# Four cross-attention layers on one core: folded weights stored in whole rows, prologue transfers in another order, three transposes inside the second query projection, weight pieces split in other phases

## The chip, the cores and the metric

One core of a Trainium2 chip runs the kernel. The metric is the device time of one execution in microseconds (us), as the median of several runs. TensorE (PE) multiplies matrices, VectorE (DVE), ScalarE (ACT) and GpSimd (POOL) do elementwise work, and the sync engine's queue (SP) issues most transfers.

## The reference

Four cross-attention layers follow one another on `x` (4 batches, 1024 tokens, 512 features); each attends to a context of 64 tokens of 1024 features. Layers 0 and 2 are "grouped", layers 1 and 3 are "masked":

```python
# grouped (layers 0 and 2)
xn = rmsnorm(x, norm_w)
q = (xn @ wq)                       # 16 heads of 32
k, v = cond @ wk, cond @ wv         # 4 key heads of 32
attn = softmax(q k^T / sqrt(32))
x = x + (attn v) @ wo
# masked (layers 1 and 3)
q, k, v = x @ Wq, ctx @ Wk, ctx @ Wv      # 16 heads of 64
logits = q k^T / 8 + column bias of four token positions, by mask
x = x + softmax(logits) v @ Wo + bo
```

## The kernel before

Every product of matrices that needs precision is made of three PE passes (`three`, lines 372 to 376): the operands are split into a high part (ACT, a copy that rounds to fp32r) and a low part (a subtraction on DVE or POOL), and high x high, high x low and low x high are summed. So each operand passes ACT and then DVE or POOL before PE can use it.

**Prologue.** For the masked layers the query weights are multiplied into the keys and the output weights into the values ahead of time ("folding"): 32 steps n (`MASKED`), each one projection of keys or values (`m_made`, 24 matmuls of 256 columns) and one fold (`folding`, 12 matmuls of 512 columns into four PSUM banks). ACT and DVE empty the four banks into staging buffers (`taken_out`), and SP stores them to DRAM: 256 KB each, to `s_fm` (folded query weights, n 0 to 7 and 16 to 23) or to `s_fn` (folded output weights). Staging buffers are used again two steps of a kind later, after the store has landed (`f_st`). SP issues all of it in program order: the loads of the raw weights (`w_load`, `f_load`), the grouped keys and values (`g_store`), the folded weights (`f_store`), the first block of x into `ring`. The last 8 of the 32 steps are interleaved with the first attention phase.

**Main part.** There are 8 iterations `it`: 2 layer pairs x 4 batches. Each has four phases of 8 steps u (four groups of 128 tokens x two halves of the heads): phases 0 and 1 are the grouped layer for the first and second block of 512 tokens, phases 2 and 3 the masked layer. While PE makes the scores of phase k, it also transposes the finished probabilities of phase k-1 (`transposes`, into the bank `TB`; phases 0 and 3 alternate with `MX`), multiplies them by the values (`product`), and in phases 1 and 2 adds the output projection (`out_part`, eight pieces per phase). A transposed block goes through ACT (`pt_hi`) and DVE (`pt_lo`) before its product and before `TB` can be used again. Softmax of a step: ACT copies the scores (`copied`), DVE takes the maximum (`evac`), POOL subtracts it (`less_max`), ACT takes the exponential (`exp`), DVE sums and takes the reciprocal (`sums`), POOL multiplies (`norm`); in phases 2 and 3 DVE does the first part alone.

Before phases 0 and 1 there is the query projection (`q_bound`): four chunks c of 12 matmuls; chunk c needs the chunk of x split by ACT (`x_hi`) and POOL (`x_lo`). The output weights of the grouped layer are split during phase 1: ACT `ws_hi(it, 4 + u)` after `copied(it, 1, u)`, POOL `ws_lo(it, 4 + u)` after `less_max(it, 1, u)`. `out_part` for j waits for piece j of them:

```python
                if ph == 1 and part == 0:
                    pe.wait_ge(S["ws_lo"], 8 * it + 4 + j + 1)
```

The folded weights come back in 16 pieces of 256 KB per iteration through the four slots of `ring`, and are split by `part_hi` (ACT) and `part_lo` (DVE for pieces 0 to 3, POOL for the others): pieces 0 to 3 are used by steps u 0 to 3 of phases 2 and 3, pieces 4 to 7 by steps u 4 to 7, pieces 8 to 15 by the products of phase 3 and of the next phase 0. After phase 1, DVE adds the layer's output to x (`xnew`), ACT and then POOL and DVE split it (`xb_hi`, `xb_lo`), and the scores of phase 2 (`scores(it, 2, 0)`) need all four chunks of it.

Each engine works through its own program in order; the order of the calls in the code below is therefore the order of the work on that engine. PE's iterations 1 to 7 are one hardware loop.

## Time and profile before

| | |
|---|---|
| median of 3 runs | 1669.56 us (1668.48 to 1671.2) |
| profiled execution, its own time | 1669.71 us |
| span in the profile | 1667.9 us |
| mean granted clock of TensorE | 0.995 of full speed |
| PE busy | 1597.5 us (96%) |
| DVE, POOL, ACT busy | 1089.3, 882.1, 769.7 us |

The profile is of one execution. The span is what the trace covers; the execution's own time is 1.8 us longer. Matmuls are pipelined and their ends are modelled, so a matmul of 512 columns shows about 0.39 us while the next one starts 0.23 us after it: an idle time before a matmul is therefore about 0.16 us shorter in the records than the lateness of its start.

### The profile page before, as it was taken

What the parts mean: (1) busy time and instruction counts of PE and PEld (TensorE: products, weight loads), DVE (VectorE), ACT (ScalarE), POOL (GpSimd) and SP (SyncE); (2) the same over time, 40 slices, a digit from 0 to 9 for tenths busy, and PEclk for the clock granted to TensorE, in tenths of its full rate; (3) what the DMA queues carried; (4) which work ended last, traced back from release to release, by engine and by line L of the source; (5) the groups of instructions that cost most, each with busy time, mean ns of one, the idle gap of its engine ahead of it and who ended that gap; (6) DMA issues with size and microseconds to landing.
All of it is one profiled execution on the core that took longest, in us unless ns stands there. A gap on an engine that the chain in (4) does not pass through costs nothing.

```text
span 1667.9 us, 25208 instructions
## 1 busy us (share of the span) xinstructions
PE 1597.5 (96%) x8160; PEld 1330.8 (80%) x8160; DVE 1089.3 (65%) x1825; ACT 769.7 (46%) x1353; POOL 882.1 (53%) x809
## 2 busy tenths in 40 slices
PE   7999999999999999999999999999999999999998
PEld 6988887788778877878777877887787877787786
DVE  6676468764676567655876567656865587657764
ACT  4565566334643364435642463336533563246331
POOL 4040446645745575556755575557455665557430
PEclk9999999999999999999999999999999999999999
DMA  9999562121311222121222231122112221222101
GB/s 321 276 341 339 187 228 89 51 68 67 132 39 52 102 83 76 45 96 61 105 57 65 77 120 40 50 102 95 64 51 90 82 89 51 65 76 95 43 9 51
DMA packets 118451, 172.18 MB, mean 103 GB/s; under 512 B 35760, under 2 KB 69040, under 8 KB 112176
## 3 DMA queue, kind: packets, MB, share of 16 engines
q1 hardware_dynamic: 115424, 153.16, 28.1%
q10 hardware_dynamic: 2736, 16.78, 2.5%
q8 instruction: 78, 1.28, 0.3%
q14 instruction: 53, 0.43, 0.1%
q0 software_dynamic: 160, 0.53, 0.1%
HBM read 118.53 MB, written 51.91 MB: 102 GB/s over the span
## 4 chain that ended last, share of the span: by engine, by line
PE 45%; issue 25%; POOL 17%; DVE 5%; ACT 4%; SPq 2%; DMA 2%; POOLq 0%; DVEq 0%; ACTq 0%
PE OB L374 10%; PE OB L376 9%; PE OB L375 9%; POOL foldN L1243 4%; PE SB L374 3%; PE SB L376 3%; PE SB L375 3%; PE TB L488 2%; POOL xqhl L1228 2%; POOL xhl L1249 2%; POOL foldM L1243 2%; POOL wqo L1146 2%; POOL wraw L1139 1%; POOL prob L1220 1%; DVE pT L905 1%
## 5 line engine op out<-in xcount | busy, mean ns | idle before, releaser
L1220 POOL TENSOR_TENSOR prob<-prob,small 128x512 f32<-128x512 f32 x256 | 281.4, 1102 | 392.4 <-DVE small L1023 392.4
L775 ACT ACTIVATE pT<-TB 128x512 fp32r<-128x512 f32 x192 | 114.0, 594 | 280.3 <-PE TB L488 280.3
L1004 DVE SCALAR_TENSOR_TENSOR prob<-SB,aux 128x512 f32<-128x512 f32 x128 | 88.2, 689 | 198.3 <-PE SB L376 198.3
L1214 POOL TENSOR_TENSOR prob<-prob,small 128x512 f32<-128x512 f32 x128 | 133.9, 1046 | 151.3 <-DVE small L998 151.3
L374 PE MATMUL SB<-foldM,xhl 128*128 128x512 f32 x512 | 202.0, 395 | 9.0 <-POOL foldM L1243 6.9
L374 PE MATMUL OB<-pT,foldN 128*128 128x512 f32 x512 | 205.8, 402 | 3.8 <-DVE pT L905 3.7
L905 DVE TENSOR_TENSOR pT<-TB,pT 128x512 fp32r<-128x512 f32 x192 | 127.9, 666 | 117.4 <-ACT pT L775 116.8
L375 PE MATMUL OB<-pT,foldN 128*128 128x512 f32 x512 | 200.5, 392 | 0.0
L376 PE MATMUL OB<-pT,foldN 128*128 128x512 f32 x512 | 200.4, 391 | 0.0
L376 PE MATMUL SB<-foldM,xhl 128*128 128x512 f32 x512 | 199.7, 390 | 0.0
L375 PE MATMUL SB<-foldM,xhl 128*128 128x512 f32 x512 | 199.3, 389 | 0.0
L998 DVE TENSOR_REDUCE small<-prob 128x8 f32<-128x512 f32 x128 | 87.4, 683 | 137.2 <-ACT prob L768 136.2
L747 ACT ACTIVATE prob<-prob 128x512 f32<-128x512 f32 x128 | 80.9, 632 | 207.5 <-DVE prob L1010 206.8
L768 ACT ACTIVATE prob<-SB 128x512 f32<-128x512 f32 x128 | 76.5, 598 | 167.0 <-PE SB L376 166.9
L488 PE MATMUL TB<-ident,prob 128*128 128x128 f32 x768 | 117.5, 275 | 18.1 <-DVE pT L905 18.0
L374 PEld LDWEIGHTS SB<-foldM,xhl 128*128 128x128 f32 x512 | 96.1, 188 | 38.7 <-POOL foldM L1243 10.2
L488 PEld LDWEIGHTS TB<-ident,prob 128*128 128x128 f32 x768 | 90.3, 140 | 43.5 <-DVE pT L905 25.7
L374 PE MATMUL OB<-xqhl,wqo 128*128 128x512 f32 x256 | 105.6, 412 | 17.4 <-POOL xqhl L1228 16.1
L1228 POOL TENSOR_TENSOR xqhl<-ring,xqhl 128x512 fp32r<-128x512 f32 x64 | 82.2, 1295 | 66.1 <-ACT xqhl L754 66.0
L374 PEld LDWEIGHTS OB<-pT,foldN 128*128 128x128 f32 x512 | 96.7, 189 | 22.0 <-DVE pT L905 4.0
L376 PEld LDWEIGHTS OB<-pT,foldN 128*128 128x128 f32 x512 | 96.5, 189 | 21.1
L376 PEld LDWEIGHTS SB<-foldM,xhl 128*128 128x128 f32 x512 | 96.1, 188 | 20.4
(159 smaller groups left out, 4121.8 us busy)
## 6 DMA issues: line engine op xcount, KB each, us to landing
prob<-in_wkvM_dram SPq DMA_DIRECT2D x32, 512.0 KB, 5.7
ring<-s_fm SPq DMA_DIRECT2D x64, 256.0 KB, 2.6
ring<-s_fn SPq DMA_DIRECT2D x64, 256.0 KB, 2.6
out_dram<-x ACTq DMA_DIRECT2D x15, 1024.0 KB, 3.9
wraw<-in_wqG_dram SPq DMA_DIRECT2D x8, 1024.0 KB, 4.8
s_fm<-prob SPq DMA_DIRECT2D x32, 256.0 KB, 5.5
s_fn<-x SPq DMA_DIRECT2D x32, 256.0 KB, 5.0
ring<-in_xT_dram SPq DMA_DIRECT2D x32, 256.0 KB, 3.2
```

Of the source, the lines that this page charges most:

```text
L374: pe.matmul(out, a_hi, b_hi, start=start, stop=False)
L375: pe.matmul(out, a_hi, b_lo, start=False, stop=False)
L376: return pe.matmul(out, a_lo, b_hi, start=False, stop=stop)
L488: last = pe.transpose(out[:, tt * P:(tt + 1) * P], pr[:, tt, t * P:(t + 1) * P], ident[:, :])
L775: act.activation(pT[:, t % 2, 0, :], t_bank(ph, t)[:, :], ACT.Copy).then_inc(S["pt_hi"], 1)
L905: return dve.tensor_tensor(out, psum, hi.bitcast(F32), ALU.subtract)
L998: dve.reduce_max(hmax[u % 2], own, AX_X).then_inc(S["maxed"], 1)
L1004: dve.scalar_tensor_tensor(out=own, in0=bank, scalar=M_SCALE, in1=row, op0=ALU.mult, op1=ALU.add).then_inc(S["biased"], 1)
L1214: pool.tensor_tensor(own, own, hmax[u % 2].unsqueeze(2).broadcast_to([P, HH, KEYS]), ALU.subtract).then_inc(S["evac"], 1)
L1220: pool.tensor_tensor(own, own, rsum[u % 2].unsqueeze(2).broadcast_to([P, HH, KEYS]), ALU.mult).then_inc(S["normed"], 1)
L1228: pool.tensor_tensor(xqhl[:, 1, c % 2, :], ring[:, c, :], xqhl[:, 0, c % 2, :].bitcast(F32), ALU.subtract).then_inc(S["x_lo"], 1)
L1243: pool.tensor_tensor(fold_part(i, 1), ring[:, i % 4, :], fold_part(i, 0).bitcast(F32), ALU.subtract).then_inc(S["fb_lo"], 1)
```

## The change

- The folded query weights are stored to `s_fm` with each partition's 2 KB in one piece (before: four pieces of 512 bytes); they are read back as pieces of 512 bytes instead of whole rows.
- In the prologue SP issues the loads in another order: two of the first four `f_load`s and the query weights `wraw` later, `w_load(4)` and `w_load(5)` ahead of the grouped stores, the first block of x at n = 20 instead of 24. ACT splits the query weights at n 12 to 15 (before 8 to 11) and the first two chunks of x at n = 20.
- In the second query projection PE makes transposes 0, 1, 2 ahead of chunks 1, 2, 3, and products 0 and 1 ahead of chunks 2 and 3. Phase 1 then starts with its scores, and from u = 1 makes transpose u+2, product u+1 and output piece u-1. The first transpose of phase 2 moves ahead of the last scores of phase 1.
- In iterations 1 to 7 weight pieces 0 to 3 are loaded before the second block of x and split in phase 0 (before: phase 1); pieces 4 to 7 are loaded ahead of the next query weights and split two at a time at the start of phase 2, and the scaling of the next query weights moves up.
- POOL: `norm(it, 3, 5)` moves behind the first two `x_lo` of the next iteration, and `x_lo(it, 1, 2)` ahead of `norm(it, 0, 7)`.

The core of the diff:

```diff
-        sFM = nc.dram_tensor("s_fm", (PAIRS, BATCH, 2, DC, P, HALF), F32, kind="Internal").ap()
+        sFM = nc.dram_tensor("s_fm", (PAIRS, KC, DC, P, BATCH, P), F32, kind="Internal").ap()
...
-                        sp.dma_start(sFM[lp, :, t // 4, o, :, (t % 4) * P:(t % 4 + 1) * P].rearrange("b p n -> p b n"),
-                                     staged(n, o).rearrange("p (b n) -> p b n", b=BATCH)).then_inc(f_st[n % 2], 16)
+                        sp.dma_start(sFM[lp, t, o].rearrange("p b n -> p (b n)"), staged(n, o)).then_inc(f_st[n % 2], 16)
...
             for n in range(4):
                 w_load(n)
-                f_load(n)
+                if n < 2:
+                    f_load(n)
...
-            sp.dma_start(wraw[:, :, :], wqG[0]).then_inc(S["ld_w"], 16)
-            for i in range(GROUP):
-                g_store(0, i)
-            for n in range(2):
-                sp.dma_start(wG[:, n], wkvG[1, n]).then_inc(wg_in[n], 16)
             for n in range(4, MASKED + 9):
                 if n < MASKED:
                     w_load(n)
+                if n == 5:
+                    for i in range(GROUP):
+                        g_store(0, i)
+                    for i in range(2):
+                        sp.dma_start(wG[:, i], wkvG[1, i]).then_inc(wg_in[i], 16)
+                    f_load(2)
+                    f_load(3)
...
+                if n == 11:
+                    sp.dma_start(wraw[:, :, :], wqG[0]).then_inc(S["ld_w"], 16)
...
-                if n == 24:
+                if n == 20:
                     sp.wait_ge(f_st[0], 4 * 64)
...
+                def half(hf, c):
+                    return sFM[lp, 4 * hf:4 * hf + 4, c, :, b, :].rearrange("t p n -> p t n")
...
                     for c in range(DC):
-                        ring_load(4 + c, x_of(1)[:, c, :])
+                        half_load(0, c, ("x_lo", value(8, c + 1)), ("x_sq", value(8, c + 1)))
                     sp.wait_ge(S["stored0"], value(16))
                     sp.dma_start(X[0][:, :, :], x_of(0)).then_inc(S["ld_x0"], 16)
-                for c in range(DC):
-                    ring_load(8 + c, sFM[lp, b, 0, c])
+                    for c in range(DC):
+                        ring_load(c, x_of(1)[:, c, :], ("fa_lo", value(4, c + 1)))
...
                 sp.dma_start(X[1][:, :, :], x_of(1)).then_inc(S["ld_x1"], 16)
+                for c in range(DC):
+                    if first:
+                        half_load(1, c, ("fa_lo", c + 1))
+                    else:
+                        half_load(1, c, ("x_lo", value(8, c + 5)), ("x_sq", value(8, c + 5)))
...
 # tensor engine, q_bound
                 for c in range(DC):
-                    if c == DC - 1 and not (first and ph == 0):
-                        transposes(it, ph, 0, first)
-                        if ph == 0:
-                            transposes(it, ph, 1, first)
+                    if ph == 1 and c > 0:
+                        transposes(it, 1, c - 1, first)
+                        if c > 1:
+                            product(it, 1, c - 2, first)
+                    elif c == DC - 1 and not first:
+                        transposes(it, 0, 0, first)
+                        transposes(it, 0, 1, first)
...
             def grouped_grouped(it, first):
 
-                for u in range(STEPS):
-                    if u > 0:
-                        transposes(it, 1, u, first)
-                        product(it, 1, u - 1, first)
-                    if u >= 3:
-                        out_part(it, 1, (u - 3) // 2, (u - 3) % 2)
+                scores(it, 1, 0, first)
+                for u in range(1, STEPS):
+                    if u + 2 < KC:
+                        transposes(it, 1, u + 2, first)
+                    if u + 1 < KC:
+                        product(it, 1, u + 1, first)
+                        out_part(it, 1, (u - 1) // 2, (u - 1) % 2)
+                    if u == STEPS - 1:
+                        transposes(it, 2, 0, first)
                     scores(it, 1, u, first)
-                product(it, 1, KC - 1, first)
-                out_part(it, 1, 2, 1)
-                transposes(it, 2, 0, first)
                 out_part(it, 1, 3, 0)
                 out_part(it, 1, 3, 1)
...
 # scalar engine: prologue, phase 0, phase 1, phase 2
-                if 8 <= n < 8 + DC:
-                    ws_hi(0, n - 8)
+                if 12 <= n < 12 + DC:
+                    ws_hi(0, n - 12)
+                if n == 20:
+                    for i in range(PAIRS):
+                        act.wait_ge(g_st[i], (BATCH + 2) * 16)
+                    act.wait_ge(S["bias_b"], PAIRS)
+                    x_hi(0, 0, 0, True)
+                    x_hi(0, 0, 1, True)
...
+                    if not first and u < 4:
+                        part_hi(it, u, first)
...
+                copied(it, 1, 0)
+                ws_hi(it, DC)
+                for u in range(1, STEPS):
+                    if u + 2 < KC:
+                        pt_hi(it, 1, u + 2)
+                    if u % 2 == 0:
+                        ot_hi(2 * it, u // 2)
+                    if u == STEPS - 1:
+                        pt_hi(it, 2, 0)
                     copied(it, 1, u)
-                    if u == STEPS - 1:
-                        ot_hi(2 * it, 3)
-                    if u > 0:
-                        exp(it, 1, u - 1)
+                    exp(it, 1, u - 1)
                     if u < DC:
                         ws_hi(it, DC + u)
...
-                    part_hi(it, 4 + s - 1)
+                    if s <= 2:
+                        part_hi(it, 2 + 2 * s, first)
+                        part_hi(it, 3 + 2 * s, first)
+                    elif s <= 6:
+                        part_hi(it, 5 + s, first)
...
 # vector engine: phase 0, phase 1
+                    if not first and u < 4:
+                        part_lo(it, u)
...
                 pt_lo(it, 1, 0)
+                pt_lo(it, 1, 1)
+                pt_lo(it, 1, 2)
+                ot_lo(2 * it, 0)
                 q_lo(it, 1)
...
+                    if u == STEPS - 1:
+                        pt_lo(it, 2, 0)
                     evac(it, 1, u, first)
-                    if u == STEPS - 1:
-                        ot_lo(2 * it, 3)
-                    if u > 0:
-                        sums(it, 1, u - 1, first)
-                    if 3 <= u < 3 + DC:
+                    sums(it, 1, u - 1, first)
+                    if first and 3 <= u < 3 + DC:
                         part_lo(it, u - 3)
-                pt_lo(it, 2, 0)
...
 # gpsimd
                 if not first:
+                    norm(it - 1, 3, STEPS - 3)
                     norm(it - 1, 3, STEPS - 2)
...
+                x_lo(it, 1, 2, first)
                 norm(it, 0, STEPS - 1)
-
-                x_lo(it, 1, 2, first)
...
-                for u in range(STEPS):
-                    part_lo(it, 4 + u)
-                    if u >= DC and nxt is not None:
-                        ws_scale(it + 1, u - DC, nxt)
-                    if u < STEPS - 2:
-                        norm(it, 2, u)
+                for u in range(STEPS - 2):
+                    if u < 2:
+                        part_lo(it, 4 + 2 * u)
+                        part_lo(it, 5 + 2 * u)
+                    else:
+                        part_lo(it, 6 + u)
+                        if nxt is not None:
+                            ws_scale(it + 1, u - 2, nxt)
+                    norm(it, 2, u)
```

## Rows read from the trace of the kernel before

**Rows 1.** The page, busy time of each engine and share of the span.
```profile
PE 1597.5 (96%) x8160; PEld 1330.8 (80%) x8160; DVE 1089.3 (65%) x1825; ACT 769.7 (46%) x1353; POOL 882.1 (53%) x809
```

**Rows 2.** Waits of PE: line, releaser, us in total, times, longest.
```profile
PE TB L488 <- DVE pT L905: 18.0, 40, 0.7
PE OB L374 <- POOL xqhl L1228: 16.1, 15, 3.0
...
PE SB L374 <- POOL foldM L1243: 6.9, 8, 0.9
```

**Rows 3.** Timeline of PE, prologue: start, us, engine, line; in brackets idle before and releaser.
```profile
32.14 0.47 PE L374 MATMUL OB<-foldM,pT 128*128 128x512 f32 x1 [3.61 <-ACT ring L696]
...
165.76 0.47 PE L374 MATMUL OB<-foldM,pT 128*128 128x512 f32 x1 [1.88 <-ACT x L696]
...
173.38 0.75 PE L374 MATMUL OB<-xqhl,wqo 128*128 128x512 f32 x1 [3.04 <-POOL xqhl L1228]
```

**Rows 4.** Timeline of SP, prologue: the issues of four weight loads.
```profile
20.81 3.02 SPq L202 DMA_DIRECT2D prob<-in_wkvM_dram  x4
```

**Rows 5.** Timeline of ACT, prologue.
```profile
27.92 1.06 ACT L670 ACTIVATE foldN<-prob 128x1024 fp32r<-128x1024 f32 x1 [7.08 <-DMA prob<-in_wkvM_dram]
...
165.01 1.09 ACT L696 ACTIVATE x<-OB 128x512 f32<-128x512 f32 x2 [1.94 <-DMA s_fm<-x]
```

**Rows 6.** Windows: us busy, instructions of PE, PEld, DVE, ACT, POOL; clock; DMA share; GB/s.
```profile
100.00:130.00 30.00, 29.29 (x190) 26.63 (x189) 21.13 (x31) 16.08 (x29) 10.76 (x19) 1.00 0.98 331
130.00:175.00 45.00, 39.53 (x225) 34.29 (x224) 27.26 (x41) 24.70 (x45) 3.14 (x3) 0.94 1.07 337
```

**Rows 7.** Windows behind two stalls of PE, columns as in group 6.
```profile
33.47:36.88 3.41, 3.41 (x10) 2.54 (x9) 3.37 (x6) 2.42 (x5) 3.24 (x8) 0.50 0.92 250
...
1453.42:1456.83 3.41, 3.41 (x9) 2.63 (x9) 2.32 (x5) 0.63 (x1) 1.95 (x3) 0.50 0.31 96
```

**Rows 8.** Timeline of PE at two starts of an iteration.
```profile
1093.25 0.49 PE L374 MATMUL OB<-xqhl,wqo 128*128 128x512 f32 x1 [1.95 <-POOL xqhl L1228]
...
1453.14 0.59 PE L374 MATMUL OB<-xqhl,wqo 128*128 128x512 f32 x1 [1.91 <-POOL xqhl L1228]
```

**Rows 9.** Timeline of PE, iteration 3, start of phase 1.
```profile
789.62 0.37 PE L374 MATMUL SB<-kG,foldM 128*128 128x256 f32 x1
...
790.77 0.48 PE L374 MATMUL MX<-pT,vG 128*128 128x512 f32 x1
791.56 0.28 PE L374 MATMUL SB<-kG,foldM 128*128 128x256 f32 x1
...
793.00 0.66 PE L488 MATMUL TB<-ident,prob 128*128 128x128 f32 x4 [0.59 <-DVE pT L905]
...
797.25 0.40 PE L374 MATMUL OB<-foldN,wqo 128*128 128x512 f32 x1
```

**Rows 10.** Timeline of all engines, the same stretch: what POOL does.
```profile
792.13 1.04 POOL L1214 TENSOR_TENSOR prob<-prob,small 128x512 f32<-128x512 f32 x1 [0.80 <-DVE small L998]
...
793.13 1.29 POOL L1146 TENSOR_TENSOR wqo<-wraw,wqo 128x512 fp32r<-128x512 f32 x1
```

**Rows 11.** The page's costliest groups: busy, mean ns of one, idle before.
```profile
L775 ACT ACTIVATE pT<-TB 128x512 fp32r<-128x512 f32 x192 | 114.0, 594 | 280.3 <-PE TB L488 280.3
...
L1214 POOL TENSOR_TENSOR prob<-prob,small 128x512 f32<-128x512 f32 x128 | 133.9, 1046 | 151.3 <-DVE small L998 151.3
...
L905 DVE TENSOR_TENSOR pT<-TB,pT 128x512 fp32r<-128x512 f32 x192 | 127.9, 666 | 117.4 <-ACT pT L775 116.8
```

**Rows 12.** Timeline of all engines, end of phase 1 of iteration 3.
```profile
818.08 2.47 DVE L1034 TENSOR_TENSOR x<-OB,x 128x512 f32<-128x512 f32 x4
...
819.50 3.01 POOL L1249 TENSOR_TENSOR xhl<-x,xhl 128x512 fp32r<-128x512 f32 x2 [1.18 <-ACT xhl L789]
...
820.86 0.50 PE L374 MATMUL SB<-foldM,xhl 128*128 128x512 f32 x1 [0.15 <-POOL xhl L1249]
```

**Rows 13.** Timeline of PE in phase 2 of iteration 3.
```profile
844.48 0.50 PE L374 MATMUL SB<-foldM,xhl 128*128 128x512 f32 x1 [0.85 <-POOL foldM L1243]
```

More of the change, by code:

```diff
@@ L696, in taken_out, with x_hi @@
                     act.activation(staged(n, o), FB[o][:, :], ACT.Copy).then_inc(S["ev_a"], 1)
+            def x_hi(it, ph, c, first):
+                a = 2 * it + ph
+                act.wait_ge(ld_ring[c], 16 * (6 * it + (ph + 1 if first else 2 * ph + 1)))
+                if not (first and ph == 0 and c < 2):
+                    act.wait_ge(S["qchunk"], 4 * a + c - 1)
+                act.activation(xqhl[:, 0, c % 2, :], ring[:, c, :], ACT.Copy).then_inc(S["x_hi"], 1)
+                if c >= 2:
+                    act.wait_ge(S["sq_added"], 3 * a + 1)
+                elif not (first and ph == 0):
+                    act.wait_ge(S["sq_added"], 3 * a - 1 + c)
+                act.activation(xsq[:, c % 2, :], ring[:, c, :], ACT.Square).then_inc(S["x_sq"], 1)
             def ws_hi(it, i):
```

87 lines of the change are left out of this document (35 added, 52 removed).

## The prediction, made before the changed kernel ran

> **What bounds the kernel.** The page's busy times come first: PE is busy 96% of the span, no other engine over 65% [rows 1]. So the end is set by PE's instructions, which the change leaves the same in number and shape, and by the moments in which PE waits. I then read PE's waits in total, and where in an iteration each stands. Three groups matter: transposes that wait for the low part of the block before them (18.0 us), query projections that wait for x from POOL (16.1 us), and scores that wait for folded weights from POOL (6.9 us) [rows 2]. A wait costs more than its idle time, since about 0.16 us hide behind the modelled end of the matmul before it.
>
> The second loss is the clock. After the 3.61 us wait at 32.14 [rows 3] a stretch of 3.41 us ran at half speed, 1.2 instead of 2.4 GHz, and so did one behind the 1.91 us wait at 1453.14 [rows 7, 8]. Such a stretch costs a busy PE 1.7 us. The 1.95 us wait at 1093.25 was not followed by one: the clock's row at its place stays at 1.00. Waits of three microseconds are thus dear, waits near two sometimes, waits under one never here.
>
> **Prologue.** The 3.61 us wait: ACT idled 7.08 us for weight load 4 and so was late with the bank PE wanted [rows 5]; SP had issued that load only at 20.81, behind the grouped stores [rows 4]. The change issues it when DVE has freed its buffer, some 8 us earlier. The two fold loads that now go later are wanted near 28 and are issued near 21; a load takes 7 us there (20.81 to 27.92), so this just fits. Gain 3.8 us and the 1.7 us of clock. Later waits come from ACT, which waits 1.94 us for a store to free its staging buffer before 165.01 [rows 5]; they cost PE 1.88 us at 165.76 [rows 3], 0.7 and 0.5 us at two places before, and one more slow stretch. And 3.04 us at 173.38, with a third slow stretch, because the first x chunks are split only after the last fold's eviction; at n = 20 ACT has room for those four pieces of 0.6 us, so this wait goes. All together 3.8 + 0.9 + 0.7 + 2.0 + 3.2 = 10.6 us of waits and 3 x 1.7 = 5.1 us of clock, 15.7 us. Moving `ws_hi` and `wraw` to later steps costs nothing, hidden by folds that don't use them. Some waits will stay, since the transfers are near their limit (DMA share 0.98 and 1.07 [rows 6]): I take 12 us, bounds 5 and 16.
>
> The whole rows are a part of that. The stretch with 512-byte stores moved 337 GB/s at a share of 1.07, the one with 2 KB stores 331 at 0.98 [rows 6]: 7% less per unit of DMA time, some 6 us over the 95 us of such stages. The Trainium skill ("DMA: Bandwidth & Descriptors", Specifications) says that 512 B are enough for line rate; by that the stores gain nothing. The GB/s alone agree with it, the share doesn't; what would follow is a rival below. The reads in 512-byte pieces lie in the main part with its DMA share near 0.2 and are wanted tens of microseconds later: nothing.
>
> **One iteration, removed.** In phase 1 five transposes wait, because only a product and scores stand between them while a block needs ACT (0.59 us) and DVE (0.67 us) behind their other work [rows 9, 11]: 0.75 (the 0.59 idle at 793.00 and what hides), 0.88, 0.62, 0.16 and 0.40 us of lateness, and 0.2 us at three of the products behind them, 3.4 us. In the new order a chunk of 2.7 us, or an output piece, stands between any two. The wait of chunk 2 of that projection (0.35 us) is covered by two transposes and a product. The wait at 844.48 for weight piece 7 (0.85 idle, 1.0 us late) goes: POOL now makes pieces 4 to 7 ahead of its second `norm` [rows 13]. Sum 4.75 us. The moved POOL `norm(it, 3, 5)` gains nothing: at six starts of an iteration PE's own loop turn takes over 1.1 us before its first record, while x is ready by then; and in iteration 1, where there is no turn, chunk 2 waits for a chain that begins with the last scores.
>
> **One iteration, added.** First: output piece 0 moves from u = 3 to u = 1, but it needs weight piece 4 from POOL, whose place in POOL's order is unchanged: after `less_max(it, 1, 0)`, which comes at 792.13, then the piece, 793.13 to 794.42 [rows 10]. That is 4.80 us after phase 1's scores start at 789.62. In the new order PE wants it after the scores (0.80), a transpose (0.35) and a product (0.79, 790.77 to 791.56), thus after 1.94 us [rows 9]. PE stands 2.9 us, 2.7 by the record. Before, it came at 797.25, 2.8 us after the piece was done. Around it, ot and weight piece 5 arrive 0.2 to 0.3 us late in three rounds: 0.8 us.
>
> Second: the end of phase 1. Before, a product, an output piece and a transpose (2.1 to 2.8 us) stood between the last scores and the last two output pieces; now nothing does, and the last two scores are only one transpose apart. From the end R of scores(1,6), DVE and ACT have to do in turn: copy 0.6, maximum 0.7, sums 0.9, low part of the transposed block 0.65, maximum 0.7; POOL `less_max` 1.05; ACT exponential 0.7, first high part of x 0.65; POOL low part 1.3; with handovers 7.5 us [rows 11, 12]. PE's own work from R to scores(2,0) is a transpose 0.4, scores 0.75, output pieces 2.8, a transpose 0.35, a product 0.8: 5.1 us. It waits 2.3 us, and 0.35 more at chunks 2 and 3, whose low parts are slow while POOL and DVE work together (3.01 us for POOL's two [rows 12]). Before, the same place cost 0.8 us. The transpose behind it: +0.2. Together +2.05 us.
>
> Added 2.9 + 0.8 + 2.05 = 5.75 us, removed 4.75: +1.0 us. In phase 0, ACT and DVE take one weight piece more per step for four steps (0.6 and 0.7 us in a step of 3.9 us, in which PE has 0.5 us or more to spare at each product): nothing; without that cover 0.1 us a step. Seven iterations +7.0; iteration 0, which still splits its pieces in phase 1, +2.4 (0.7 us later at the end). Sum +9.4 us, bounds -10 and +29, with the two new waits (4.95 us together, eight times) half or one and a half times as long.
>
> **Clock.** Both new waits (2.7 and 2.2 us idle, 16 in all) lie between those that sometimes and those that always brought the slow stretch. I take 9 of 16, each 1.7 us less 0.4 that other engines catch up: +11.7 us, bounds 0 and 25.
>
> **Sum.** -12 + 9.4 + 11.7 = +9.1 on the profiled execution's own 1669.7, which is the median to 0.2: 1679 us. Its own range is 1673 to 1688 us.
>
> **Rivals.**
> A. The clock stays up at the new waits. For it: 1.95 us without a fall [rows 8]. Against: every wait above 3 us fell. -12 + 9.4: 1667 us. Chance 0.2.
> B. Faster: the end of phase 1 doesn't lengthen, because PE reaches the last scores late and the elementwise engines early after the 2.9 us wait. It decides if the chain from R is under 5.9 us instead of 7.5. Then an iteration is 1.05 us shorter, 8.4 in all, the clock costs 8 x 0.75 x 1.5 = 9, and -12 - 8.4 + 9 gives 1658 us. Against: the chain's terms are single rows and R is the last scores but one. Chance 0.22.
> C. The prologue stays bound by transfers: stores in whole rows relieve nothing, and what PE gains at 32.14 it stands later at `f_st`. Only the x wait and half of the rest goes, -6: 1685 us; with nothing gained 1691. For it: DMA shares near 1 [rows 6]. The Trainium skill's 512-byte rule ("DMA: Bandwidth & Descriptors", Specifications) would lead here. Chance 0.13.
> The forecast has 0.45.
>
> **Range and chances.** From B's 1658 to between C's two, 1690, is left out less than 2 in 10. Within 0.2% (1666.2 to 1672.9 us, about what a measurement of this kernel can tell from no change) lie half of A and a little of the forecast: 0.14. Faster: B and the rest of A, 0.30. Slower: 0.56.
>
> **What would show it.** No wait near 32, 166 and 173 us for the prologue. Per iteration a wait of PE at the first `OB<-foldN,wqo` of phase 1, released by POOL `wqo`, near 2.7 us, and one at the first `SB<-foldM,xhl` of phase 2, near 2.2 us; transposes in phase 1 with next to none; none for `foldM` from POOL. Clock windows at half behind about nine of them. I am wrong if the time between starts of iterations falls below the 180 us of before (1093.25 and 1453.14 are two iterations apart [rows 8]), or the two new waits are under 1 us.

## The result and the profile after

The changed kernel takes 1678.0 us (median of 20 runs, 1670.9 to 1680.7), the kernel before, in 20 runs beside it, 1669.8 (1668.2 to 1673.8). The ratio is 1.0043, 95% interval 1.0034 to 1.0052: slower by 0.4%, 1 us from the predicted 1679. The profiled execution of the changed kernel took 1680.7 us (span 1678.9), that of the kernel before 1669.7. So the traces differ by 11 us, the medians by 8. Differences between kernels below are of medians unless a ratio is named. One execution of the run `fill` ran at a mean granted clock of 0.75 (1991 us) and is left out of its median.

That the sum came out is partly luck, as the experiments below show: the terms for the main part together were 8 to 9 us too large and one was missing at 7 to 9 us, and they cancel.

The page's busy time of PE after, which answers to [rows 1]: the same 8160 instructions show 5.7 us more.

```profile
PE 1603.2 (95%) x8160; PEld 1346.9 (80%) x8160; DVE 1095.6 (65%) x1825; ACT 768.0 (46%) x1353; POOL 885.0 (53%) x809
```

PE's waits after: line waited for, releaser, us in total, times, longest. They answer to [rows 2].

```profile
PE OB L385 <- POOL wqo L1175: 19.1, 7, 2.7
PE SB L385 <- POOL xhl L1278: 14.8, 7, 2.1
PE OB L385 <- DVE x L1061: 10.1, 12, 1.9
...
PE OB L385 <- issue: 4.8, 2, 2.7
...
PE SB L385 <- issue: 3.0, 1, 3.0
```

The 18.0 us of transposes that waited and the 6.9 us for folded weights are gone. In their place stand the two waits that were forecast: output piece 0 for weight piece 4 (19.1 us in seven iterations; the eighth is one of the two put down to "issue"), and the first scores of phase 2 for the low part of the new block (14.8, and 3.0 in iteration 0).

The timeline of PE in iteration 3 shows both: start, us, engine, line, and in brackets the idle time before.

```profile
789.91 0.37 PE L385 MATMUL SB<-kG,foldM 128*128 128x256 f32 x1
...
791.62 0.40 PE L387 MATMUL MX<-pT,vG 128*128 128x512 f32 x1
794.74 0.50 PE L385 MATMUL OB<-foldN,wqo 128*128 128x512 f32 x1 [2.73 <-POOL wqo L1175]
...
818.44 0.40 PE L387 MATMUL MX<-pT,vG 128*128 128x512 f32 x1
820.96 0.50 PE L385 MATMUL SB<-foldM,xhl 128*128 128x512 f32 x1 [2.12 <-POOL xhl L1278]
```

From 789.91, when the scores begin, to 794.74 are 4.83 us; the prediction had 4.80 from [rows 9, 10]. What the prediction did not have stands at the loop turn, where the next iteration starts:

```profile
909.76 0.39 PE L387 MATMUL SB<-foldM,xhl 128*128 128x512 f32 x1
911.98 0.49 PE L385 MATMUL OB<-xqhl,wqo 128*128 128x512 f32 x1 [1.83 <-DVE x L1061]
912.31 0.53 PE L386 MATMUL OB<-xqhl,wqo 128*128 128x512 f32 x1
912.64 0.63 PE L387 MATMUL OB<-xqhl,wqo 128*128 128x512 f32 x1
913.07 0.63 PE L385 MATMUL OB<-xqhl,wqo 128*128 128x512 f32 x1
```

The releaser that the profile names is now DVE's `x` (`xnew`), where it was POOL's `xqhl` in [rows 8]; experiment 7 shows that PE waited for neither. From 912.64 the matmuls start 0.43 us apart instead of 0.23. The window behind it (columns as in [rows 6]) shows the clock at half, that is 1.2 GHz:

```profile
912.40:915.81 3.41, 3.41 (x10) 2.64 (x9) 2.35 (x6) 0.63 (x1) 1.68 (x2) 0.50 0.01 2
```

The trace of before has 5 stretches of this kind, 3.41 us each, that of after 20: 7 behind the wait for weight piece 4 (of 8), 6 at five of the eight waits at the start of phase 2, 5 behind the six loop turns, and 2 at the end of the program, the last of which begins 1.9 us before the span ends. Before, one of the six turns had one.

What a stretch costs can be read from the 20 executions of the changed kernel alone. The slowest took 1680.7 us at a mean granted clock of 0.980, the fastest 1670.9 at 0.988. A straight line through all 20 gives 1.1 us for each 0.001 of clock, and 0.001 of 1679 us is the 1.7 us that one stretch at half speed takes from the clock. So a stretch costs about 1.1 us of time in this kernel; this is an estimate from the 20 pairs of time and clock.

The prologue, where the trace answers to [rows 3, 6]: no wait at 32, 166 or 173 us, and one new one.

```profile
115.46 0.47 PE L385 MATMUL OB<-pT,foldM 128*128 128x512 f32 x1 [2.00 <-ACT x L710]
```

```profile
50.00:100.00 50.00, 50.00 (x323) 45.59 (x322) 38.27 (x56) 31.11 (x56) 21.93 (x32) 1.00 0.99 335
100.00:130.00 30.00, 28.00 (x180) 25.38 (x179) 20.80 (x30) 17.72 (x33) 15.10 (x23) 1.00 1.02 370
130.00:175.00 45.00, 44.93 (x266) 39.67 (x265) 29.32 (x42) 26.53 (x47) 13.93 (x14) 1.00 0.84 296
```

The second query projection of iteration 0 begins at 223.3 us, before at 237.9: 14.6 us earlier. From there the changed kernel loses 25.6 us, to end 11 later.

### The profile page after: what moved, and what is told of

It reads as the page before. It is cut to its first block, busy times and chain, and to the rows that moved or that the text cites. A ratio compares the mean times of both kernels' runs of the same rounds, so it can differ in the third digit from the quotient of the medians.

```text
span 1678.9 us, 25256 instructions
## 1 busy us (share of the span) xinstructions
PE 1603.2 (95%) x8160; PEld 1346.9 (80%) x8160; DVE 1095.6 (65%) x1825; ACT 768.0 (46%) x1353; POOL 885.0 (53%) x809
## 4 chain that ended last, share of the span: by engine, by line
PE 75%; issue 9%; DVE 7%; POOL 6%; ACT 1%; DMA 1%; DVEq 0%; SPq 0%; POOLq 0%; ACTq 0%
PE OB L385 14%; PE OB L387 13%; PE OB L386 13%; PE SB L385 8%; PE SB L387 7%; PE SB L386 7%; PE TB L502 3%; PE MX L385 2%; PE MX L387 2%; PE MX L386 2%; PE MX L502 1%; DVE x L1059 1%; DVE x L1061 1%; POOL wqo L1175 1%; POOL prob L1243 1%
## 5 line engine op out<-in xcount | busy, mean ns | idle before, releaser
L385 PE MATMUL SB<-foldM,xhl 128*128 128x512 f32 x512 | 204.0, 398 | 18.2 <-POOL xhl L1278 14.8
L387 PE MATMUL SB<-foldM,xhl 128*128 128x512 f32 x512 | 203.0, 397 | 0.0
L386 PE MATMUL SB<-foldM,xhl 128*128 128x512 f32 x512 | 202.7, 396 | 0.0
L385 PEld LDWEIGHTS SB<-foldM,xhl 128*128 128x128 f32 x512 | 97.9, 191 | 44.2 <-POOL xhl L1278 17.9
L385 PE MATMUL OB<-foldN,wqo 128*128 128x512 f32 x256 | 104.8, 409 | 22.5 <-POOL wqo L1175 19.1
L385 PE MATMUL OB<-xqhl,wqo 128*128 128x512 f32 x256 | 106.2, 415 | 14.1 <-DVE x L1061 10.1
L387 PEld LDWEIGHTS SB<-foldM,xhl 128*128 128x128 f32 x512 | 98.1, 192 | 21.0
L386 PEld LDWEIGHTS SB<-foldM,xhl 128*128 128x128 f32 x512 | 98.1, 192 | 20.1
```

The costliest lines, as they stand in the source:

```text
L385: pe.matmul(out, a_hi, b_hi, start=start, stop=False)
L386: pe.matmul(out, a_hi, b_lo, start=False, stop=False)
L387: return pe.matmul(out, a_lo, b_hi, start=False, stop=stop)
```

## The experiments

The kernel before ran on the same chip beside each of them, with medians of 1668.5 to 1669.6 us; each ratio is against those runs.

**1. Only the prologue: `prologue_only`.** The kernel before with the new order of the prologue's transfers, the whole-row stores of `s_fm` and the early split of x; its iterations are untouched.

```diff
 for n in range(4):
     w_load(n)
-    f_load(n)
+    if n < 2:
+        f_load(n)
...
-    if n == 24:
+    if n == 20:
         sp.wait_ge(f_st[0], 4 * 64)
         for c in range(DC):
             sp.dma_start(ring[:, c, :], xT[0, 0, :, c, :]).then_inc(ld_ring[c], 16)
```

> The kernel before with only the prologue of the change: stores of the folded query weights in whole rows (and their reads in 512-byte pieces), the order of loads, the query weights split at n 12 to 15, the first two chunks of x split at n = 20. Theory: the second query projection of iteration 0 began 14.6 us earlier in the changed kernel than before, and nothing of that depends on the main part: 1655 us, 1653 to 1658. Rival: reads in 512-byte pieces cost time in the main part (they land in 5.8 instead of 2.6 us); then above 1660 us.

Measured: 1656.3 us, ratio 0.9929 [0.9912, 0.9945]. Iterations 1 to 6 take 179.6 to 181.4 us, as before (179.7 to 181.4). The prologue is worth 12 us, as predicted; the rest of the change thus costs 22 us (19 by the ratios). Rival C, which had this part at 0 to -6 us, falls here.

**2. Whole rows or 512 bytes: `prologue_old_rows`.** The same kernel, with `s_fm` stored and read as before.

```diff
-sp.dma_start(sFM[lp, t, o].rearrange("p b n -> p (b n)"), staged(n, o))
+sp.dma_start(sFM[lp, :, t // 4, o, :, (t % 4) * P:(t % 4 + 1) * P].rearrange("b p n -> p b n"),
+             staged(n, o).rearrange("p (b n) -> p b n", b=BATCH))
```

> The kernel before with the changed order of the prologue's transfers and the early split of x, but with the folded weights stored as before, in pieces of 512 bytes, and read back in whole rows; the run prologue_only stored whole rows of 2 KB and gave 1656.3 us. Theory of the prediction: the 512-byte stores take more of the transfer engines than the whole rows, so part of the 13 us comes back: 1661 us (1658 to 1665), with waits of PE in the prologue. Rival C, the rule that pieces of 512 bytes are already efficient: 1656 (1655 to 1657.5). What would surprise: under 1655, the 512-byte reads of the loop cost more than the stores gained.

Measured: 1661.0 us, ratio 0.9943 [0.9931, 0.9954]. The medians are 4.7 us apart, the ratios 0.14%, which is 2.3 us and within their intervals, so the times alone don't show a difference; the profiled executions are 6.2 us apart, 6.0 of them already at the start of iteration 1. The windows show why. First the kernel with whole rows, then the one with 512-byte pieces, the same 50 us:

```profile
50.00:100.00 50.00, 50.00 (x323) 45.59 (x322) 37.44 (x56) 31.05 (x56) 21.83 (x32) 1.00 0.98 335
```

```profile
50.00:100.00 50.00, 50.00 (x323) 45.64 (x322) 36.62 (x55) 29.59 (x54) 21.44 (x32) 1.00 1.06 335
...
130.00:175.00 45.00, 44.03 (x256) 38.54 (x256) 28.02 (x41) 26.00 (x46) 12.92 (x12) 1.00 1.06 317
```

Both move 335 GB/s, but with the small pieces that takes 8% more of the DMA engines' time (1.06 against 0.98). Up to 100 us that costs PE nothing; later stores land late, and PE waits at 109, 117.5 and 168 us (1.3, 2.9 and 1.1 us late), where the kernel with whole rows has one wait, at 115 (2.0 us late). So the traces bear out the prediction's reading of [rows 6], at 2 to 6 us where it had 6; the time by itself does not settle it. The Trainium skill ("DMA: Bandwidth & Descriptors", Specifications) gives 512 B as enough for line rate. The equal GB/s do not contradict it, but PE is busy all through both windows, so they show only what its work asks for; the share is what differs.

**3. x as late as before: `prologue_x_late`.** `prologue_only` with the x loads at masked step 24 again, and their high parts behind the last eviction.

```diff
-    if n == 20:
+    if n == 24:
         sp.wait_ge(f_st[0], 4 * 64)
         for c in range(DC):
             sp.dma_start(ring[:, c, :], xT[0, 0, :, c, :]).then_inc(ld_ring[c], 16)
...
 taken_out(EARLY - 1)
+x_hi(0, 0, 0, True)
+x_hi(0, 0, 1, True)
```

> The run prologue_only (1656.3 us) with the transfer of the first iteration's x issued at masked step 24 and its high parts made behind the last evacuation, as in the kernel before; the order of the first loads and the whole-row stores stay changed. The prediction priced the early x at the two waits at the end of the prologue, 1.88 and 3.04 us, and the half-speed stretches behind them. Expected: the waits come back, about 5 us and 1 to 2 us of clock: 1662 us (1660 to 1665). Rival: with the stores in whole rows the transfers are through early enough and x is no longer late: 1657 us (1655 to 1658).

Measured: 1656.7 us, ratio 0.9929 [0.9916, 0.9942]. The rival is right on the time, but for another reason. The wait for x is there as expected, with a half-speed stretch behind it:

```profile
161.62 0.76 PE L384 MATMUL OB<-xqhl,wqo 128*128 128x512 f32 x1 [3.32 <-POOL xqhl L1241]
162.19 0.63 PE L385 MATMUL OB<-xqhl,wqo 128*128 128x512 f32 x1
```

What is missing is the wait at 115 us (2.00 us in the changed kernel, 1.8 in `prologue_only`). The two kernels differ only in when x is loaded and split. The rows of SP and ACT show how the early load makes that wait, first in `prologue_only`: SP issues the x loads ahead of a store, and ACT waits 4.80 us for the landing of a store of that buffer.

```profile
102.83 2.11 SPq L280 DMA_DIRECT2D ring<-in_xT_dram  x4
...
105.57 2.52 SPq L220 DMA_DIRECT2D s_fn<-x  x4
```

```profile
114.72 1.08 ACT L706 ACTIVATE x<-OB 128x512 f32<-128x512 f32 x2 [4.80 <-DMA s_fn<-x]
```

The same in `prologue_x_late`, where the store is issued 2.1 us and ACT's copy begins 3.3 us earlier:

```profile
103.46 2.52 SPq L220 DMA_DIRECT2D s_fn<-x  x4
```

```profile
111.45 1.09 ACT L706 ACTIVATE x<-OB 128x512 f32<-128x512 f32 x2 [1.86 <-DMA s_fn<-x]
```

The second query projection of iteration 0 begins at 223.29 us in `prologue_only`, at 225.89 here and at 237.87 in the kernel before. So the early x exchanges one wait for a shorter one, worth 2.6 us in these traces; the medians, 0.4 us apart, don't show it.

**4. Weight piece 4 earlier: `early`.** The changed kernel with that piece split by ACT and POOL before the first step of phase 1, behind the last x parts.

```diff
 x_hi(it, 1, 3, first)
+ws_hi(it, DC)
...
 copied(it, 1, 0)
-ws_hi(it, DC)
...
 x_lo(it, 1, 3, first)
+ws_lo(it, DC)
...
-if u < DC:
+if 0 < u < DC:
     ws_lo(it, DC + u)
```

> The changed kernel, but ScalarE and GpSimd split output weight piece 4 right after the last chunk of x of the second query projection (ws_hi behind x_hi(it, 1, 3), ws_lo behind x_lo(it, 1, 3)) instead of behind the first scores of phase 1. Theory: the 2.9 us lateness at the first output piece of each iteration goes (8 x 2.9 = 23 us) and with it the six half-speed stretches behind it (6 x 1.2 = 7 us); the wait at the first scores of phase 2 (2.1 us idle) stays. 1648 us, 1643 to 1654. Rival: the wait only shows a shortage of the elementwise engines in phase 1; then the transposes or products of the rounds behind it wait instead and the time stays above 1670 us.

Measured: 1642.0 us, ratio 0.985 [0.9831, 0.9869], 36 us under the changed kernel (32 by the ratios). The first wait is gone, the second is as long as it was. The trace has 5 half-speed stretches instead of 20.

```profile
PE SB L385 <- POOL xhl L1278: 14.8, 7, 2.1
PE OB L385 <- DVE x L1061: 9.8, 12, 1.9
```

The wait itself is 8 x 2.9 = 23 us. The other 9 to 13 go to the clock: the trace has 15 stretches fewer, which at 1.1 us each would be 16. Taking away one wait also took away stretches at places where the waits stayed: one turn of six has one now, and its wait is no shorter.

**5. Output pieces one round later: `later`.** The changed kernel, with PE's order of output pieces in phase 1 shifted by one step, so that other work covers the wait for weight piece 4.

```diff
 if u + 1 < KC:
     product(it, 1, u + 1, first)
-    out_part(it, 1, (u - 1) // 2, (u - 1) % 2)
+if u >= 2:
+    out_part(it, 1, (u - 2) // 2, (u - 2) % 2)
```

> The changed kernel, but all output pieces of phase 1 come one round later (piece u-2 in round u from u = 2), so that one of them stands between the first transpose of phase 2 and the last scores of phase 1. Theory: the wait for weight piece 4 shrinks from 2.7 to about 1.2 us idle, the one at the first scores of phase 2 from 2.1 to about 0.8, a transpose in round 2 waits 0.6 us; about 2.4 us per iteration less, 19 in all, and most of the 11 half-speed stretches behind the two waits go, 13 us: 1646 us, 1642 to 1656. Rival: the end of phase 1 is set by the total work of the elementwise engines, not by PE's order there; then the second wait stays near 2.1 us and the time is 1655 to 1662 us.

Measured: 1635.2 us, ratio 0.9808 [0.9788, 0.9828]. Waits of PE:

```profile
PE OB L385 <- DVE x L1062: 11.6, 13, 2.0
PE SB L385 <- POOL xhl L1279: 9.0, 7, 1.3
PE TB L502 <- DVE pT L931: 7.8, 17, 0.7
```

The first wait is gone whole, the second is 1.3 us instead of 2.1: output piece (2, 1) now stands between the last two scores. This one line of PE's order is worth 43 us against the changed kernel (39 by the ratios), and it leaves both kernels behind.

**6. PE kept busy in the waits: `fill`.** The changed kernel with ten matmuls of no use ahead of the wait for weight piece 4 and nine ahead of the first scores of phase 2. They write banks that the next real matmul opens anew.

```diff
 if ph == 1 and part == 0:
+    if j == 0:
+        open_out(it, ph, 0)
+        for _ in range(10):
+            pe.matmul(OB[0][:, :], vG[:, 0, 0, :], kG[:, 0, 0:512], start=True, stop=True)
     pe.wait_ge(S["ws_lo"], 8 * it + 4 + j + 1)
...
+if ph == 2 and u == 0:
+    for _ in range(9):
+        pe.matmul(out[:, :], vG[:, 0, 0, :], kG[:, 0, 0:512], start=True, stop=True)
```

> The changed kernel with PE kept at work during its two new waits: ten matmuls of 512 columns ahead of the wait for weight piece 4 and nine ahead of the first scores of phase 2, into banks that the next product overwrites; their results are not used. Nothing that is needed comes earlier. Theory: the waits remain in length but the half-speed stretches behind them go, 11 of them at about 1.2 us: 1666 us, 1661 to 1671. Rival: the stretches cost nothing, as other engines are late anyway: 1678 us or, as the extra matmuls delay what is behind them, more.

Measured: 1661.4 us, ratio 0.9959 [0.9946, 0.9973]; the traced execution, 1667.6 us, was the slowest of the five and has 6 half-speed stretches. From the second query projection to the first scores of phase 2 its iterations 1 to 7 take 45.7 us, as long as the one of the changed kernel that has no stretch in this part (45.67). So nothing useful was made earlier, and yet the time fell by 17 us (14 by the ratios, 13 between the traced executions). For the 14 stretches fewer in the trace, 13 us are 0.9 each, a little under the 1.1 of the 20 executions. Below, a stretch is taken at 1.1 us, with 0.9 as the lower bound.

**7. The moved normalisation: `later_norm_back` and `after_norm_back`.** The prediction gave the move of `norm(it, 3, 5)` behind the next iteration's first low parts of x nothing. Here it alone is undone, first on top of `later`, then in the changed kernel.

```diff
 if not first:
-    norm(it - 1, 3, STEPS - 3)
     norm(it - 1, 3, STEPS - 2)
...
-if u < STEPS - 3:
-    norm(it, 3, u)
+norm(it, 3, u)
```

> The run later with the normalisation of step 5 of phase 3 back in its old place, at the end of phase 3 on POOL instead of behind the first two low parts of x of the next iteration. The prediction gave this move nothing: 1635.2 us (1633.5 to 1637), the loop turn as long as with it. Rival: at its old place it holds up the low parts of x, and the loop turn is longer by up to 0.9 us each time, 1642 (1638 to 1645).

> The changed kernel with only one thing undone: the normalisation of step 5 of phase 3 is back at the end of phase 3 on POOL, where the kernel before has it, and no longer behind the first two low parts of x of the next iteration. Theory, from the run later_norm_back, where this gave 3.7 us: at the moved place the low part of x on POOL runs beside DVE's subtraction for phase 3 step 6 (1.51 us in the changed kernel against 0.70 before), xnew is 0.4 us later, PE's wait at the loop turn is 2.0 us instead of 1.6 and brings a half-speed stretch in 5 of 6 turns instead of 1 of 6. Expected: the wait at the turn back at 1.5 to 1.7 us, released by POOL, about four stretches fewer, 7 x 0.35 + 4 x 1.2 = 7 us less: 1671 us (1668 to 1675). The prediction's own claim, that the move changes nothing: 1678 us.

Measured: 1631.6 us, ratio 0.9772 [0.976, 0.9785], 3.7 under `later`; and 1669.4 us, ratio 1.0002 [0.9992, 1.0012]: with this one move undone the changed kernel is level with the kernel before. The move thus costs 8.6 us (6.8 by the ratios) in the changed kernel, and 3.7 (6.0) on top of `later`. The timelines of DVE at the turn, first of the changed kernel, then of `after_norm_back`. The first row of each is the subtraction of step 6, which stands ahead of `xnew`, the second row:

```profile
906.19 1.52 DVE L1035 TENSOR_TENSOR prob<-prob,small 128x512 f32<-128x512 f32 x1
...
908.45 2.72 DVE L1061 SCALAR_TENSOR_TENSOR x<-OB,aux,x 128x512 f32<-128x512 f32 x4
```

```profile
901.08 0.69 DVE L1035 TENSOR_TENSOR prob<-prob,small 128x512 f32<-128x512 f32 x1
...
902.52 2.72 DVE L1061 SCALAR_TENSOR_TENSOR x<-OB,aux,x 128x512 f32<-128x512 f32 x4
```

and of POOL, in the same order:

```profile
904.61 2.54 POOL L1257 TENSOR_TENSOR xqhl<-ring,xqhl 128x512 fp32r<-128x512 f32 x2
907.11 1.75 POOL L1265 TENSOR_TENSOR sqsum<-xsq 128x512 f32<-128x512 f32 x1
908.82 1.04 POOL L1249 TENSOR_TENSOR prob<-prob,small 128x512 f32<-128x512 f32 x1
```

```profile
902.68 1.05 POOL L1249 TENSOR_TENSOR prob<-prob,small 128x512 f32<-128x512 f32 x1 [3.14 <-DVE small L1048]
903.68 2.53 POOL L1257 TENSOR_TENSOR xqhl<-ring,xqhl 128x512 fp32r<-128x512 f32 x2
906.16 1.30 POOL L1265 TENSOR_TENSOR sqsum<-xsq 128x512 f32<-128x512 f32 x1
```

Where the normalisation stays, POOL waits 3.14 us for DVE's sum and is idle while DVE subtracts (0.69 us). Moved, POOL's low part of x falls on that subtraction, and it takes 1.52 us, at each of the seven starts of an iteration; POOL's sum behind it takes 1.75 instead of 1.30. In `after_norm_back`, as in the kernel before, it is the subtraction of step 7 that is long (1.41 us at 906.59); that one stands behind `xnew`. The Trainium skill ("SBUF — State Buffer", SBUF: two separate sides) describes a port pair that a DVE instruction with two SBUF inputs and a POOL instruction hold in turn, one of them blocked; these rows agree. `xnew` behind it is late, too: it starts 1.3 us before PE's last matmul of the iteration (909.76), in `after_norm_back` 2.1 us before it (904.64).

But `xnew` is not what PE's start waits for, though the profile puts the wait down to it. The first matmul of an iteration needs only the first of `xnew`'s four instructions:

```python
elif c == 0:
    pe.wait_ge(S["xnew"], 4 * (k - 2) + j + 1)
```

That one ended at 909.20, before PE's last matmul of the old iteration had started, and POOL's low part of x for this chunk at 905.9; PE starts the new iteration at 911.98. In `after_norm_back` POOL's part for this chunk ended at 904.99, and PE starts at 906.48. So in both kernels the turn is PE's own, as the prediction had it, and yet it is longer with the move. Over the six turns it is late by 2.01 us on average in the changed kernel and by 1.77 in `after_norm_back`; in all six traces with the move the average is 1.90 to 2.05, in all eight without it 1.67 to 1.84. At the start of iteration 1, where there is no turn, PE waits 0.4 us more at the third chunk of x (2.0 us late instead of 1.6) and 0.3 us less at the first, so nothing is lost there. The six turns together are 1.5 us; for the rest there are 20 stretches against 12. Why PE's turn grows is not shown by any run.

**8. The end of phase 1: `tail_early`, `tail_later`, `tail_pt`, `xnew_first`.** Four attempts on the second wait. The first two move the last two output pieces ahead of the last scores, and `xnew` and the parts of the new block ahead of the last evacuation, on top of `early` and of `later`.

```diff
 if u == STEPS - 1:
     transposes(it, 2, 0, first)
+    out_part(it, 1, 3, 0)
+    out_part(it, 1, 3, 1)
 scores(it, 1, u, first)
-out_part(it, 1, 3, 0)
-out_part(it, 1, 3, 1)
```

> The same reordering of the end of phase 1 on top of the run early (weight piece 4 split before the first step of phase 1), where the second wait was 2.28 us late. Theory: 8 times about 2 us of waiting go, and the half-speed stretches behind that wait with them (about 3 more us): 1624 us (1616 to 1632). Rival: the evacuation of the last scores is late by as much: 1642 (1636 to 1648).

> Output pieces of phase 1 one round later as in the run later, and in addition the last two output pieces stand before the last scores of phase 1 instead of behind them; xnew, the hi and lo parts of the new block on all engines come before the last scores' evacuation. Theory: the second wait (1.45 us late in that run, the chain out piece, xnew, hi part, lo part on POOL) is then covered by the last scores of about 3.9 us, so PE's wait before the first scores of phase 2 falls under 0.5 us and 8 times about 1.2 us go: 1626 us (1620 to 1633). Rival: the same work lands on DVE, ACT and POOL in front of the last scores' evacuation, which is then late for the second scores of phase 2 by as much: no gain, 1635 (1632 to 1640).

Measured: 1659.0 us, ratio 0.992 [0.99, 0.994], and 1652.7 us, ratio 0.9887 [0.9866, 0.9908]: 17 us slower than the kernels they were built on. The wait before the first scores of phase 2 is gone and a longer one has come at the second transposes (2.8 us idle in iterations 1 to 7), with more half-speed stretches: 14 against 5 in `tail_early`, 13 against 5 in `tail_later`. PE, then ACT, in `tail_later`:

```profile
807.93 0.40 PE L387 MATMUL SB<-foldM,xhl 128*128 128x512 f32 x1
811.13 0.66 PE L502 MATMUL TB<-ident,prob 128*128 128x128 f32 x4 [2.81 <-DVE pT L931]
```

```profile
808.85 0.72 ACT L775 ACTIVATE prob<-prob,small 128x512 f32<-128x512 f32 x1 [2.49 <-POOL prob L1244]
809.47 0.58 ACT L793 ACTIVATE pT<-TB 128x512 fp32r<-128x512 f32 x1
```

ACT stands 2.49 us in its exponential of step 7, for POOL's subtraction of step 7, and the block that PE needs (`pT`) is queued behind it. Both theory and rival missed that queue. `tail_pt` mends it: on top of `tail_later` and the normalisation back, exponential and sum of step 7 stand behind that block.

```diff
 for s in range(1, STEPS):
     pt_hi(it, 2, s)
+    if s == 1:
+        exp(it, 1, STEPS - 1)
```

> The run later_norm_back (1631.6 us) with the last two output pieces before the last scores of phase 1, xnew and the parts of the new block before the last scores' evacuation, and exponential and sum of phase 1 step 7 behind the part of the first transposed tile of phase 2 on ACT and DVE. In tail_later the second wait was gone and a wait of 2.98 us stood at the second transposes of phase 2, since ACT and DVE reached that tile only behind exponential and sum of step 7, which waited for POOL. Theory: with that queue order mended both waits are gone, 8 x 1.4 us: 1620 us (1614 to 1627). Rival: the maximum of step 7 and the normalisations on POOL are still late, and the transposes that need the second half of the probabilities, or the second scores of phase 2, wait instead: 1630 to 1640 us.

Measured: 1634.6 us, ratio 0.9788 [0.9776, 0.9801]. Both waits are gone and two of 0.8 and 0.9 us have come, at the second and third transposes; 3 us above `later_norm_back`. The last one leaves PE's order alone and takes only the sum, the exponential and the normalisation out of the queue ahead of `xnew` and the new block's parts:

```diff
-exp(it, 1, STEPS - 1)
 xb_hi(it, 1)
+exp(it, 1, STEPS - 1)
...
 xnew(it, 1)
 xb_lo(it, 1)
+sums(it, 1, STEPS - 2, first)
 sums(it, 1, STEPS - 1, first)
```

> The run later_norm_back (1631.6 us) with xnew and the parts of the new block at the end of phase 1 ahead of the sum of step 6 on DVE, the exponential of step 7 on ACT and the normalisation of step 6 on POOL; PE's order unchanged. There xnew began 0.9 us after its first output piece, behind maximum of step 7 and sum of step 6 on DVE, and the second wait was 1.43 us late. Theory: the second wait is the length of this queue on the elementwise engines; with the sum out of it the wait falls to about 0.6 us, 7 or 8 times 0.8 us: 1625 us (1621 to 1629). Rival, from tail_pt, where both waits went and others of 1 us each came: the sum and the normalisation are late instead and the first transposes or scores of phase 2 wait for them: 1631.5 us (1630 to 1634).

Measured: 1631.3 us, ratio 0.9779 [0.9766, 0.9792]. The second wait falls from 1.3 to 0.17 us, and the transposes behind it wait 1.10:

```profile
796.52 0.50 PE L385 MATMUL SB<-foldM,xhl 128*128 128x512 f32 x1 [0.17 <-POOL xhl L1281]
...
801.06 0.65 PE L502 MATMUL TB<-ident,prob 128*128 128x128 f32 x4 [1.10 <-DVE pT L931]
```

The theory had the place and the length of the wait right and the gain wrong; the rival's time (1631.5) was measured. Three orders, `tail_pt`, `xnew_first` and `later_norm_back`, thus end within 3 us. This fits the reading that at the change from phase 1 to 2 the chain on DVE, ACT and POOL sets the time, and that an order only chooses at which instruction PE stands; no run shortens that chain, so it is not shown. The best kernels are `later_norm_back` and `xnew_first`, 2.3 and 2.2% under the kernel before.

## Why the prediction was right, and where only its sum was

**Prologue, -12 us: right, its parts not.** -14.6 us in the trace, -12 in the medians of `prologue_only`. The wait at 32.14 went as told, and so did those for the staging buffer but for the new one at 115. The early x was priced at 3.2 us and a half-speed stretch of 1.7; undone, it costs 2.6 us in the trace and 0.4 in the medians (`prologue_x_late`), since the early transfers delay a store and bring the wait at 115. The whole rows are worth 2 to 6 us, and the estimate was 6.

**The waits of the iterations, +9.4 us: right in kind, too high in size.** In iteration 3 the first wait was 2.89 us late (forecast 2.9) and the second 2.28 (forecast 2.3, though the prediction's own terms, 7.5 and 5.1 us, leave 2.4). Three small latenesses around weight piece 5 came to 0.7 (0.8). All three removed waits went. By stages, iteration 3 of the kernel before, which starts at 732.94, against that of the changed kernel, which starts at 730.20:

| stage | before | changed | difference | prediction's terms |
|---|---|---|---|---|
| start to second query projection | 43.8 | 45.1 | +1.3, the stretch at its turn | 0 |
| to first scores of phase 2 | 44.1 | 45.7 | +1.6 | +1.95 |
| to the next start, without the longer turn | 92.0 | 90.7 | -1.3 | -1.0 |

Without the stretch that is +0.3 us an iteration, where the forecast was +1.0. The runs `prologue_only` and `after_norm_back` differ by just the main part without the moved normalisation. Their profiled spans are 14.3 us apart: 0.9 at the start of iteration 0, 3.4 in iteration 0 with one stretch (forecast 2.4 without any), and 10.1 in the other seven iterations, with about nine stretches more. At 1.1 us a stretch about 11 of the 14.3 are the clock; at 0.9, about 9. What is left for waits is 3 to 5 us, and most of it lies in iteration 0 and before it. So the term of +9.4 us is the one that was mis-sized, in its seven iterations of +1.0. Why each of the last two stages came out 0.3 us lower than its terms stays open.

**Clock, +11.7 us: right for the waits it was made for.** Forecast were nine of the 16 new waits with a stretch, at 1.3 us each. In `after_norm_back` it was nine of 16, in the changed kernel twelve; a stretch costs 0.9 to 1.1 us. Rival A, in which the clock stays up at these waits, falls. The five stretches at the turns, where before there was one, were not in the forecast; four of them go with the moved normalisation (in `after_norm_back` one turn of six has one).

**The moved normalisation, 0: wrong.** This is the step that failed: "The moved POOL `norm(it, 3, 5)` gains nothing: at six starts of an iteration PE's own loop turn takes over 1.1 us before its first record, while x is ready by then". Its reason holds: x is ready long before PE starts. The price does not. With the move the turns are on average 0.24 us longer and five of six have a stretch instead of one. How the move lengthens PE's turn stays open. The move costs 7 to 9 us (`after_norm_back`), 4 to 6 in a kernel with fewer stretches (`later_norm_back`). What the move does to DVE and POOL could have been read in the kernel before: there DVE's subtraction of step 7, which already lay beside POOL's sum (912.50 to 913.79), took twice as long as that of step 6.

```profile
907.41 0.69 DVE L1010 TENSOR_TENSOR prob<-prob,small 128x512 f32<-128x512 f32 x1
...
912.93 1.41 DVE L1010 TENSOR_TENSOR prob<-prob,small 128x512 f32<-128x512 f32 x1
```

**The sum.** Forecast -12 + 9.4 + 11.7 + 0 = +9.1. Measured, in steps of whole kernels and by their ratios to the kernel before: -12 (`prologue_only`), +12 from there to `after_norm_back` (waits and clock, where 9.4 + 11.7 = 21 were forecast), +7 for the normalisation: +7. By the medians the last two steps are +13 and +8.6. The 8 to 9 us too many and the 7 to 9 missing cancel, and that the total was hit to 1 us is luck.

**Rivals.** B falls at the point that the prediction named: the end of phase 1 is 2.28 us late, so the chain is as long as its single rows said. C falls with `prologue_only`, whose prologue gained the 12 us; what it said of the whole rows is contradicted by the traces of `prologue_old_rows`, not by the times. The sign test of the forecast held too: iterations 1 to 6 take 181.8 to 183.9 us, above the 180 of before, but most of that is the clock.

## What to carry to other kernels

A queue that has room is not free room, and a move that delays nothing on the critical path can still cost: this one was priced at nothing and took 7 to 9 us, most of it clock. Before an instruction moves on POOL, look at which DVE instructions it will lie beside, and take their durations from a row where the two already overlap. When the profile names a releaser, look in the code which count of its semaphore the wait is for, and when that count was reached. When an instruction of PE goes earlier, list what it needs from other engines and move the makers too, or put it one step later; here that one step was worth 43 us. Count each new wait of two to three microseconds twice, once as it stands and once for the clock behind it, which here was about 1 us at more than every second one.

## What the runs showed of the hardware that was not expected

Waits well under 3 us are followed by half-speed stretches, and their length alone doesn't decide it. In the changed kernel the five loop turns that were 1.95 to 2.35 us late each had one, the sixth, 1.74 late, had none. In `early` the six turns were 1.75 to 2.55 us late, and only the one of 2.05 had one. The wait of 2.9 us in the same iteration is missing there, but it alone doesn't decide it either: in `fill`, where PE works through that wait, the turns were 1.95 to 2.1 us late and three of six had a stretch, and in `early` the latest of all, 2.55 us, had none. What decides it stays open.

The turn of PE's loop is not free. In all 14 traces the first matmul of iterations 2 to 7 started 1.5 to 2.55 us late, although the first part of x and the first instruction of `xnew`, which it needs, were ready no later than 0.4 us after the last matmul of the old iteration had started. The profile shows no wait for the rest of that time, and what sets its length, which differs from turn to turn, stays open.

The reads in 512-byte pieces land later too, 3.2 us by the median in `prologue_only` (first line) against 2.6 before, where they are whole rows; in the changed kernel, which also issues them at other moments, 5.8 (second line). No wait of PE came from it.

```profile
ring<-s_fm SPq DMA_DIRECT2D x64, 256.0 KB, 3.2
```

```profile
ring<-s_fm SPq DMA_DIRECT2D x64, 256.0 KB, 5.8
```
